# A decoder layer with attention, cross-attention and four routed experts: tile sizes of the feed-forward part, first loads, and the order of two short steps

## What is computed

```
z = layernorm(x);  q, k, v = split(z @ W.T + b)                # 16 heads of 16
x = x + softmax(causal(q k.T / 4)) v
q = layernorm(x) @ Wq.T                                        # cross part, 120 context rows
mem = ctx[argmax(q ctx.T)];  k, v = split(mem @ Wkv.T)         # one k and v for all heads
x = x + (softmax(q k.T / 4) v) @ Wc.T
h = layernorm(x);  e = argmax(h @ W_router)                    # four experts, one for each row
y = gelu(h @ W1[e] + b1[e]) @ Wo + bo + h
out = x + layernorm(y) * gamma + beta
```

## Time and profile before

| | us |
|---|---|
| median of 3 runs (lowest, highest) | 3295.55 (3292.09, 3298.89) |
| the profiled execution | 3280.96 |
| its span in the profile | 3279.1 |
| PE busy in the span | 3058.4 (93%) |
| DVE busy | 2565.8 (78%) |
| ACT busy | 1753.8 (53%) |
| POOL busy | 1272.7 (39%) |
| mean granted clock of PE | 0.981 of full speed |

### The profile page before, as it was taken

The page is one execution under the profiler, slowest core; times in us unless marked ns, Lnnn a source line. Parts: engine busy times, 40 slices in busy tenths (PEclk is TensorE's granted clock), DMA queues, the critical chain, the costliest instruction groups (busy, mean ns, idle before and its releaser), DMA issues.

```text
span 3279.1 us, 78416 instructions
## 1 busy us (share of the span) xinstructions
PE 3058.4 (93%) x26632; PEld 2417.7 (74%) x26632; DVE 2565.8 (78%) x6882; ACT 1753.8 (53%) x3260; POOL 1272.7 (39%) x1773
## 2 busy tenths in 40 slices
PE   3899999999999999999999999999849999999998
PEld 2677777777777777777777777777539999999997
DVE  2687888788788888878888887888638888888886
ACT  1465555556555655555565565556424545454543
POOL 3233333333333333333333343333214545455554
PEclk8999999999999999999999999999869999999999
DMA  5665556556556655655565565566233333434341
GB/s 100 88 110 111 98 109 115 104 99 113 112 96 111 112 103 103 112 106 98 111 112 104 102 115 107 99 107 107 56 110 136 128 138 128 142 123 146 122 149 47
DMA packets 321569, 359.70 MB, mean 110 GB/s; under 512 B 62040, under 2 KB 289631, under 8 KB 321248
## 3 DMA queue, kind: packets, MB, share of 16 engines
q1 hardware_dynamic: 308384, 321.96, 47.8%
q0 software_dynamic: 12864, 33.64, 3.1%
HBM read 140.93 MB, written 46.21 MB: 57 GB/s over the span
## 4 chain that ended last, share of the span: by engine, by line
PE 85%; DVE 8%; issue 4%; DMA 1%; SPq 1%; POOL 0%; ACT 0%; DVEq 0%; POOLq 0%
PE psum L624 15%; PE psum L986 12%; PE psum L970 12%; PE psum L619 8%; PE psum L723 4%; PE psum L811 4%; PE psum L701 3%; PE psum L710 3%; PE psum L677 3%; PE psum L674 3%; PE psum L789 3%; PE psum L668 3%; DVE negmax L1207 2%; PE psum L803 2%; PE psum L827 2%
## 5 line engine op out<-in xcount | busy, mean ns | idle before, releaser
L1039 ACT ACTIVATE PA<-psum 128x512 f32<-128x512 f32 x512 | 305.9, 598 | 354.6 <-PE psum L710 350.5
L1207 DVE TENSOR_REDUCE negmax<-psum 128x2 f32<-128x512 f32 x512 | 344.2, 683 | 106.8 <-PE psum L677 99.7
L1144 ACT ACTIVATE hT_high<-psum,b_sb 128x512 fp32r<-128x512 f32 x280 | 193.2, 690 | 415.2 <-PE psum L970 393.2
L1045 ACT ACTIVATE PC<-psum 120x512 f32<-120x512 f32 x512 | 303.8, 596 | 206.4 <-PE psum L803 205.6
L1204 DVE TENSOR_REDUCE negmax<-psum 128x4 f32<-128x512 f32 x256 | 177.0, 691 | 250.0 <-PE psum L677 243.8
L1212 DVE TENSOR_REDUCE cnegmax<-psum 128x4 f32<-128x480 f32 x512 | 324.5, 644 | 7.6 <-PE psum L789 7.4
L986 PE MATMUL psum<-wo_high,hT_low 128*128 128x256 f32 x1120 | 319.8, 286 | 0.6 <-DVE hT_low L1488 0.6
L986 PE MATMUL psum<-wo_low,hT_high 128*128 128x256 f32 x1120 | 316.9, 283 | 0.0
L986 PE MATMUL psum<-wo_high,hT_high 128*128 128x256 f32 x1120 | 316.9, 283 | 0.0
L1488 DVE TENSOR_TENSOR hT_low<-hT,hT_high 128x512 fp32r<-128x512 f32 x280 | 267.0, 972 | 52.4 <-ACT hT L1145 52.4
L624 PE MATMUL psum<-zT,wqk_sb 128*128 128x256 f32 x1024 | 266.3, 383 | 2.9 <-DVE q_rest L1230 2.2
(11 more groups left out here) (211 smaller groups left out, 8255.3 us busy)
## 6 DMA issues: line engine op xcount, KB each, us to landing
QP<-q_parts SPq DMA_DIRECT2D x384, 128.0 KB
KP<-k_parts SPq DMA_DIRECT2D x384, 128.0 KB, 4.2
QC<-cq_parts SPq DMA_DIRECT2D x384, 128.0 KB, 3.9
w_high<-w_high_dram SPq DMA_DIRECT2D x35, 1024.0 KB, 5.1
w_low<-w_low_dram SPq DMA_DIRECT2D x35, 1024.0 KB, 7.0
fx<-rows_dram SPq DMA_DIRECT2D x35, 514.0 KB
x_in<-in_x SPq DMA_DIRECT2D x64, 256.0 KB, 4.7
x_res<-in_x SPq DMA_DIRECT2D x64, 256.0 KB, 5.1
```

The lines of the kernel that those rows point to most:

```text
L1039: act.activation(dst, psum[:, ST_BANKS[n % 2], :], ACT.Exp, scale=D ** -0.5).then_inc(exp_done.sem, 1)
L1045: act.activation(PC[0:M, 2 * n:2 * n + 2, :].rearrange("p h n -> p (h n)"), psum[0:M, ST_BANKS[n % 2], :], ACT.Exp, scale=D ** -0.5).then_ ...
L1144: act.activation(hT_high[:, m, :], psum[:, m % 4, :], ACT.Gelu, bias=b1_sb[:, q, m:m + 1])
L1207: dve.tensor_reduce(negmax[:, 1, h:h + 2], bank.rearrange("p (h k) -> p h k", h=2), AX_X, ALU.max).then_inc(max_done.sem, 1)
```

## The change

- The tiles: 29 full tiles (FULL_TILES = 32 - 3) first, then 9 half tiles of 256 rows (HALF_TILES = 3 x 3), 38 in all. Everything that works on a half tile takes two row blocks in place of four and 256 columns in place of 512. The weights of an expert are loaded for a half tile as for a full one. The tile loop is written out, with no hardware loop.
- The plan: 22 steps give the full tiles, SP goes on behind them; 29 more give the half tiles and where the padding goes. SP loads the rows of tile 0 before its weights, does its first step, and only then writes the padding (256 rows each, five times). The load of the first half tile waits for it.
- The first loads: the bias of q and k comes as four rows of 128 numbers into one partition, ACT reorders it there (2 copies), PE turns it (4 transposes), ACT copies it to bqk_sb. Wq, Wc and the router's weights are issued from ACT's queue; Wo, bo, gamma and beta from SP at the end of step 4. POOL's work on Wq, the clearing of a row of QC and the padding's contents move into its step 0. PE waits for the weights in step 2, in place of step 1.
- k's rest: DVE's `subtract_high` of k goes from slot 2 to slot 1, before `residual_1`; ACT's `round_rest` of k from slot 3 to slot 2; POOL's `make_low` of k to the head of its body, before the root of the second layer norm.
- The router: in `find_rows` the addition to `next_row` becomes the second of the five steps, and PE's waits go by step 2 in place of step 5.

The core of the diff:

```diff
+    FULL_TILES = B * T // TILE - (E - 1)
+    HALF_TILES = 3 * (E - 1)
+    TILES = FULL_TILES + HALF_TILES
+    def row_blocks(k):
+        return TS if k < FULL_TILES else TS // 2
...
-        N_FIRST_LOADS = 3 + 2 * KC * HP
+        N_FIRST_LOADS = 3 + 2 * KC
...
         def tile_steps(eng, body):
-            for k in range(4):
+            for k in range(TILES + 2):
                 body(k, k % 2)
-            end = TILES - 1 - (TILES - 1) % 2
-            with eng.Fori(4, end, 2) as k:
-                body(k, 0)
-                body(k + 1, 1)
-            for k in range(end, TILES + 2):
-                body(k, k % 2)
...
-            ] + [(bqk_sb[h:P:HP, w * KC + c:w * KC + c + 1], bqkT.rearrange(...)[w, h // (HP // KC), h % (HP // KC), c].unsqueeze(1))
-                 for w in range(2) for c in range(KC) for h in range(HP)] + [
+            ] + [(bias_row[:, n * P:(n + 1) * P], bqkT[:, n].unsqueeze(0)) for n in range(2 * KC)] + [
...
+                if i == 4:
+                    for dst, src in late_loads:
+                        sp.dma_start(dst, src).then_inc(late_weights_in, 16)
...
-            sp.wait_ge(plan_step, PLAN_STEPS)
-            ... (the padding's five writes)
+            def write_padding():
+                ... (the same, of TILE // 2 rows)
+            sp.wait_ge(plan_step, FULL_PLAN_STEPS)
...
+                if k == FULL_TILES:
+                    sp.wait_ge(padded, 16 * (E + 1))
+                n = row_blocks(k)
...
+                if k == 0:
+                    write_padding()
+            load_rows(0, 0)
             load_weights(0, 0)
-            sp.wait_ge(padded, 16 * (E + 1))
-            load_rows(0, 0)
...
-                pe.wait_ge(*latest((mxT_copied, i - 1, 1), (place_step, i - 5, 5), (czT_copied, i - 3, 1)))
+                pe.wait_ge(*latest((mxT_copied, i - 1, 1), (place_step, i - 5, 2), (czT_copied, i - 3, 1)))
...
-                        (w1_low[:, q, kc, cols], fzT_high[:, kc, :]),
+                        (w1_low[:, q, kc, cols], fzT_high[:, kc, rows]),
...
-                for half in range(2):
+                for half in range(row_blocks(b) // 2):
...
-                    if n == 3 and runs(i, 0):
+                    if n == 2 and runs(i, 0):
                         round_rest(i, k_rest_made, k_parts, k_rest, k_mid)
...
+            for w in range(2):
+                half = slice(w * C, (w + 1) * C)
+                copy(bias_by_dim[:, half].rearrange(...), bias_row[:, half].rearrange(...)).then_inc(bias_ordered, 1)
...
+            act.wait_ge(bias_turned, 1)
+            copy(bqk_sb[:], psum[:, 0, 0:2 * KC]).then_inc(bias_made, 1)
...
+                dve.tensor_tensor(next_row[:], psum[:, 6, NT * E:(NT + 1) * E], next_row[:], ALU.add).then_inc(place_step.sem, 1)
                 dve.wait_ge(chosen_made.sem, chosen_made.value(b))
                 dve.tensor_tensor(place[:], place[:], chosen[:], ALU.mult).then_inc(place_step.sem, 1)
...
-                dve.tensor_tensor(next_row[:], psum[:, 6, NT * E:(NT + 1) * E], next_row[:], ALU.add).then_inc(place_step.sem, 1)
...
+                    if n == 1 and runs(i, 0):
+                        subtract_high(i, k_high, k_low, k_mid, k_parts, k_rest, 7, KC, k_rest_made)
                     if n == 1 and runs(i, 2):
                         residual_1(i - 2, par)
-                    if n == 2 and runs(i, 0):
-                        subtract_high(i, k_high, k_low, k_mid, k_parts, k_rest, 7, KC, k_rest_made)
...
+                if runs(i, 0):
+                    make_low(i, k_mid, k_parts, k_rest, k_low)
                 if runs(i, 2):
                     root(i - 2, ln2_step, cmv, crstd, ln2_rstd, LN_EPS)
-                if runs(i, 0):
-                    make_low(i, k_mid, k_parts, k_rest, k_low)
...
+                if i == 0:
+                    second_constants()
```

More of the change, by code:

```diff
@@ L262, in decoder_kernel, with sent_value @@
         sent = dma_signal("sent", TS)
-        fln_step = signal("fln_step", 3 * TS)
+        def sent_value(k):
+            return 16 * sum(row_blocks(n) for n in range(k % 2, k + 1, 2))
+        fln_step = tile_signal("fln_step", 3 * TS)
         fln_rstd = signal("fln_rstd", 2)
@@ L437, in _ @@
                 (beta_sb[:], beta.broadcast_to([P, C])),
[L438 to L441, removed]
+            ]
+            assert len(first_loads) == N_FIRST_LOADS and len(late_loads) == N_LATE_LOADS
             def load_x(b, par):
@@ L930, in _ @@
             pe.wait_ge(first_weights_in, 16 * N_FIRST_LOADS)
+            pe.wait_ge(bias_ordered, 2)
+            for n in range(2 * KC):
+                last = transpose(psum[:, 0, n:n + 1], bias_by_dim[:, n * P:(n + 1) * P], ident[0:1, 0:1])
+            last.then_inc(bias_turned, 1)
             pe.wait_ge(wqk_by_dim, 2 * KC)
@@ L949, in turn_tile @@
                         pe.wait_ge(z_low_made.sem, z_low_made.value(k - 1, kc + 1))
[L950 removed]
+                    for j in range(row_blocks(k)):
                         last = transpose(psum[:, 6 + kc, j * P:(j + 1) * P], fz[:, j, kc * P:(kc + 1) * P], ident)
@@ new lines, in _ @@
+            plan(dve.tensor_copy(used_f[:], tiles_f[:]))
+            plan(dve.tensor_tensor(used_f[:, later], tiles_f[:, later], tiles_f[:, sooner], ALU.subtract))
+            plan(dve.tensor_scalar(jump[:], used_f[:], -float(TILE), float(ROOM), ALU.mult, ALU.add))
+            plan(dve.tensor_scalar(tile_row[:, full_tiles], full_nos, float(TILE), None, ALU.mult))
+            for e in range(E - 1):
+                plan(dve.tensor_scalar(past[:, e, :], full_nos, tiles_f[:, e:e + 1], None, ALU.is_ge))
+                plan(dve.scalar_tensor_tensor(tile_row[:, full_tiles], past[:, e, :], jump[:, e:e + 1], tile_row[:, full_tiles], ALU.mult, ALU.add))
+                if e:
+                    plan(dve.tensor_tensor(tile_expert[:, full_tiles], tile_expert[:, full_tiles] if e > 1 else past[:, 0, :], past[:, e, :], ALU.add))
@@ L1499, in out_statistics @@
             def out_statistics(b, rows):
-                for j in rows:
+                for j in rows[:max(0, row_blocks(b) - rows[0])]:
                     dve.wait_ge(ysum_made.sem, ysum_made.value(b, j // 2 + 1))
@@ L1504, in out_aggregate @@
             def out_aggregate(b):
-                for j in range(TS):
+                for j in range(row_blocks(b)):
                     dve.wait_ge(oln_step.sem, oln_step.value(b, j + 1))
```

231 lines of the change are left out of this document (148 added, 83 removed).

## The result

The changed kernel takes 3206.03 us (median of 4 runs, 3201.44 to 3206.65), the kernel before beside it 3293.82 (4 runs, 3288.98 to 3298.89). The ratio is 0.9733, with a 95% interval of 0.9719 to 0.9747: 88 us less by the medians, where 77 were forecast.

The account below looks back on a forecast made before the run. PE was taken to bound feed-forward, with waits for packs and router in attention and serial stretches between. Terms 29 + 18 - 4 + 17 + 0 + 4 + 13.3 = 77 us off 3295.55 gave 3218 us, range 3182 to 3252.

Parts of the forecast that it names:

- Tiles: Feed-forward part: 29 full tiles at 23.3 us and nine half tiles at 12.3 us, 29 us less.
- loses to POOL: Half tiles: DVE's loss beside POOL's additions, 4.7 us a tile, halves with the tile; unhalved, a half tile takes 14.7 us.
- Rival 2: Feed-forward: DVE's loss to POOL not halved, or ACT, DVE, PE chain sets half tiles, 14.7 us each; 3240 us, chance 0.10.
- Start: Before the first scores: fewer first loads bring them near 36.5 us, 18 us less, between 13.6 and 22.
- Late loads: Attention step 5: 1.4 MB and four issues stand ahead of its maxima and k packs, 4 us more, 0 to 8.
- Router's bank: Attention: the addition to next_row comes sooner, so PE's 0.28 us wait goes in 60 steps, 17 us less.
- rival 4: Attention: the router's wait only turns into the next one, a DVE operation later; 3235 us, chance 0.07.
- k's rest: Attention: k's middle part reaches SP sooner, but packs' landing hangs on x's issue; 0 us, from 30 less to 8 more.
- rival 1: Attention: k's packs do land sooner, 0.47 us a step, 30 us in all; 3188 us, chance 0.18.
- signs of being wrong: PE's pack wait below 0.7 us a step, half tiles over 13.5 us, or a new PE wait in each step.
- rival 3: Attention: ACT's rounding of k held by an exponential, cz 2.8 us late each step; slower, 3327 us, chance 0.03.
- Passage and end: Between attention and feed-forward the padding leaves the path, 13.3 us less; at the end fewer sends, 4 us less.

Follow-up runs that it names:

- xb first: Changed kernel with POOL's xb of a tile issued ahead of the root of the next tile in the feed-forward part: 3202.43 us, ratio 0.9726.
- the loads' run alone: Kernel before with only the change's first loads, late loads at step 4 and moved POOL clearings: 3283.2 us, ratio 0.9973.
- x behind the packs: Load of x(i+2) issued behind k's middle and low packs: on the kernel before 3242.79 us (0.9849), on the changed kernel 3157.91 us (0.9586).

## Why the prediction was right, point by point

**Tiles**, 29 forecast, 27.4 traced. 12.40 us for a half tile against 12.3, and one of 14.93; DVE's busy time in it, 10.05 + 0.85 in the forecast, is 10.79. DVE over PE was the right reading, and the run with xb first names its reason: without xb beside fz the half tile takes 11.95 us, PE's own upper price. That DVE "loses to POOL" and that half of the loss goes with the width was thus right for the sum. Rival 2 (14.7 us each) fell.

**Start**, 18 forecast, 17.6 traced: PE starts at 14.08 (forecast near 13.5), x of sequence 2 is issued at 28.38 (near 28), the first scores come at 36.73 (near 36.5). **Late loads**, 4 forecast: 5 by moving them, 8 by the loads' run alone, the upper bound, and 6.9 in the step itself. The 4 us left out what follows PE's 4.44 us for the turned row: the clock falls behind the wait, to 0.50 in the row above.

**Router's bank**, 17 forecast, 14 measured alone. In the trace 16.5 us left and 2.5 came back in other waits, most of it for V, so rival 4 is true for about a sixth of it.

**k's rest**, 0 forecast, 0 measured in both surroundings, and rival 1 fell at the size it had (30 us). The argument, that the landing hangs on x's issue, is borne out by x behind the packs, 49 and 48 us, and by the traces: from x's issue to the scores the medians are 7.73 us before, 7.76 with k's rest alone and 7.62 in the changed kernel. But that the sum came to 0 in the run of k's rest alone is partly luck. There two of the prediction's own signs of being wrong stood, the wait for packs below 0.7 us a step (0.36) and a new wait of PE in each step (V, 58 of 59); in the changed kernel neither did (0.92, and V in 14 steps). The step was incomplete: it covered cz's wait by PE's wait at slot 8 and priced it at 0.7 us; alone it is 1.6. The delay for which rival 3 looked, ACT's rounding held by an exponential, is in the trace of k's rest alone, 1.2 us; there it takes from PE's wait at the scores about what it adds to the wait for V.

The Trainium skill's page DMA: Bandwidth & Descriptors, section Queues, rings and completion order, says that each DMA engine consumes descriptors in ring order. The two runs with x behind agree with it, though they do not prove it, as x's place on SP's queue moved too: what is ahead of the packs counts, 48 to 49 us for one load of 256 KB moved. The prediction had applied the rule to what stands behind the packs, and there the runs with k's rest show nothing.

**Passage and end**, 13.3 and 4 forecast, 12.9 and 4.6 traced. Padding has left the path.

**The level.** Forecast 3218, measured 3206. The traced parts add to 74.5 where I had 77; the 12 us come from elsewhere. By medians the change gains 88. The profiled execution of before lay 13 us under its median, that of after on it, and I carried the step of 14.6 us over to after; it belonged to that one execution. The record shows what set it apart: its mean granted clock was 0.981, while the 52 runs of the kernel before beside the experiments have 0.977 in the median, and their time goes with the clock (two at 0.974 took 3302 us in the median, 19 at 0.977 took 3292, four at 0.979 took 3288). The four runs of after have 0.981 to 0.983. By an estimate from these, 0.0230 x 3294 - 0.0183 x 3206 = 17 us less clock lost between the medians, against 0.019 x 3279 - 0.017 x 3205 = 8 between the profiled executions: 9 of the 13 us in question. That the changed kernel keeps the clock because its waits are shorter fits the traces (its longest wait for packs is 1.7 us, the falls in the tiles' run stand behind 1.87 and more), but the kernel before has waits of up to 2.24 us without a fall in its own trace, so this is not shown.

## What to carry to other kernels

Where a transfer ends a wait, look first at what is issued just ahead of it on the same queue: a load that nobody needs for two steps cost 48 us here, and making the data ready sooner gave nothing while it stood there. A gain measured as nothing may be a gain and a loss that cover each other, so compare the lists of waits and not only the times, and try the edit again once the cover is gone: k's rest was worth +22 us in one kernel and -10 in the other. And compare traces stretch by stretch, with the granted clock beside each: one execution's distance from its median is not a property of the kernel to be carried over.

## What the runs showed of the hardware

VectorE's normalization of 256 columns, from SBUF, takes 409 ns in the mean with no POOL addition beside it and 844 ns with one; in the rows above two of them take 1.60 us beside a 1.29 us addition that began 0.17 us before, and 0.73 us apart. The Trainium skill's page SBUF — State Buffer, section SBUF: two separate sides, says that VectorE and GpSimd share a pair of ports as an exclusive lock, held for a whole instruction, so that the one that comes later is fully blocked; for VectorE this goes for instructions in a 2-port mode or with two inputs in SBUF. The normalization has one large input, and no row shows its mode. The rows agree in the main: 1.60 less 0.73 is 0.87 us of blocking, where 1.12 us of the addition were left when the first normalization began, by spans of POOL that are rough.

One kernel's executions on one chip spread by 18 us (3284.39 to 3302.8, 23 runs), while in the traces of kernels with the same code there the tiles take the same time (817.6 to 817.7 us in six of them), and all behind attention agrees within 2 us. The spread lies in attention, and part of it is the granted clock: in two traces of attention with the same waits but for a few us, one had no fall of the clock from 200 to 2300 us and the other, 9 us longer, seven. Each of the seven came right behind an idle time of PE of 1.87 to 2.32 us, but other such idle times, two of 1.98 and 2.06 us in the same trace among them, had none behind them.
